# Another order of the instructions in layer 1's merged stage, and the last pair chosen in two halves

## The chip, the core and the metric

The kernel runs on one core of a Trainium2 chip. The metric is the device time of one execution in microseconds. The core has five engines that run their own instruction lists in order and meet only at semaphores: TensorE (PE in the rows, PEld for its weight loads), VectorE (DVE), ScalarE (ACT), GpSimd (POOL) and SyncE (SP). A semaphore wait stops everything queued behind it on its engine.

## The reference, cut to what matters

The program is two transformer-like layers with adaptive layer norm on 2 x 2048 tokens of width 256. The change lies in the first half of layer 1, which computes, for each batch element:

```
h  = layernorm(x) * (1 + ca) + sa
xn = h / (rms(h) + 1e-8)
u, v = silu(xn @ u_w.T + u_b), silu(xn @ v_w.T + v_b)
y  = toeplitz_mix(v)               # mixes over the batch axis of size 2
x  = x + ga * ((u * y) @ o_w.T + o_b + h)
g  = layernorm(x) * (1 + cb) + sb
xn = g * rsqrt(mean(g*g) + eps) * ln_w
logits = xn @ Wg + bg              # 8 experts
the two largest logits of a token choose its experts; softmax of the two weighs them
```

The mixing runs over an axis of size 2 here, so each row of y is a sum of both batch elements' v with three numbers per channel. The experts' own products belong to the next stage. This stage ends by putting each token's row into two slots of x_slots, sorted by expert, and by zeros behind each expert's last row.

## The kernel before, in words

`layer1` is one stage of eight, all others unchanged. Its 4096 rows are cut into 8 blocks of 512 tokens (4 tiles of 128), and a pass `c` (0 to 3, `CPS` = 4, `LAST` = 3) handles a pair of blocks, one of each batch element: j = 2c and 2c + 1. Passes are software-pipelined by hand: during pass c each engine also does work for the pair before (`older`, normalising the new x, routing) and for the pair behind (`newer`, preparing xn). Each engine's list is written out in its own block, and this written order is what the change edits.

In pass c TensorE does sixteen `up` (q = 0 to 15; p_uv, two matmuls of 128x512 each; the first eight make v, the others u), then `down(c, 0)` and `down(c, 1)` (d_po, 16 matmuls of 128x256). Between them stand `turn(2, j)` (transposes of xn_all into l_pt for the logits), `scores(j)` (logits), `turn(1, j)` (transposes of l_xn for the next pass) and `ranks` (counts of chosen experts). l_pt is one buffer, so each `turn` waits for ScalarE's `copy` of the one before. `down(c, 1)` uses the same PSUM tile as `down(c, 0)` and waits until VectorE has added that into l_h (`taken`, L1653).

ScalarE does the sixteen `gate` (silu of p_uv into v_sb or u_sb, L1429), with `square_h`, `square_n` (sums of squares), `scale_h`, `scale_n` and `copy` between them. VectorE does `center_h` and `center_n` (the layer norms), `mean_square_h`, `mean_square_n`, `invert`, `weigh` (times ln_w), `blend` (builds y_sb of v_sb, L1629 and L1634), `open_gate` (times u, L1646), `take_logits`, `choose`, `place` (slots), `residual` and `spread` (the new x and its statistics). GpSimd takes the roots (`deviation`, `inverse_root`, `root_mean_square`), adds a bias to h (`bias_rows`, L1318) and scatters rows to x_slots by indirect DMA (L1333), 16 per pair. SyncE loads weights at the start and, when `tails` is known (L1786), writes ten pieces of zeros (L1304).

The waits that matter below: `blend(c)` needs gates 0 to 7; `down(c, n)` needs `open_gate(c, n)`; `ranks` needs `choose`; `place` needs `ranks`; `scores` of the last pair need `weigh`, `turn` and `copy`; `tails` needs the ranks' total. After the last pass the last pair is normalised, scored, ranked and scattered with nothing beside it.

## Time and profile before

| | us |
|---|---|
| median of 3 runs | 2784.06 (2782.41 to 2786.93) |
| profiled execution | 2783.49 |
| its span | 2781.7 |
| the four passes of the stage (1605 to 1877) | 272.1 |
| from there to the next stage's first load (1948.5) | 71.4 |

Over the whole span TensorE is busy 82%, VectorE 61%, ScalarE 46% and GpSimd 27%, but these are averages over eight stages. The changed stage runs from about 1583 us to 1948 us of the span. The rows below are from its timeline, one engine at a time, and from its windows. A row of the timeline is: start in us, length in us, engine, line, operation, what is written and what is read, shapes and count, and in brackets how long the engine had stood idle before it and who released it.

### The profile page before, as it was taken

How to read it: one execution, taken by the hardware profiler on the slowest of the kernel's cores; microseconds unless marked ns; L12 is line 12 of the kernel's file. 1: busy time of each engine (PE TensorE's matmuls, PEld its weight loads, DVE VectorE, ACT ScalarE, POOL GpSimd, SP SyncE). 2: the span in 40 equal slices, each digit the busy share in tenths (PEclk: the TensorE clock that was granted, in tenths of full speed). 3: DMA queues.
4: the chain of work that ended last, by engine and by line, in shares of the span. 5: the costliest groups of instructions: out<-in, count | busy, mean ns of one | idle time of the engine just before them, and what ended most of it. 6: DMA issues, size and time to landing. Idle time of an engine off the chain costs nothing. (4 is left out here: it accounts for less than half of the span.)

```text
span 2781.7 us, 39688 instructions
## 1 busy us (share of the span) xinstructions
PE 2294.4 (82%) x13478; PEld 1450.0 (52%) x13478; DVE 1704.9 (61%) x2578; ACT 1276.2 (46%) x2419; POOL 750.3 (27%) x600
## 2 busy tenths in 40 slices
PE   3982899999999999997699677782799999999940
PEld 1771333333333333333577544452688888888840
DVE  4777867777666767752688757664355554545544
ACT  1330365666656676674233233321455555555520
POOL 2456001011010100000455411434233332323346
PEclk8995799999999999999899888895899999999975
DMA  4348906062442600001100100002443443443324
GB/s 157 119 145 130 254 6 144 5 142 29 118 50 98 115 2 2 2 2 43 53 0 0 29 0 1 31 31 98 169 171 122 146 150 124 136 160 120 128 63 130
DMA packets 139297, 238.37 MB, mean 86 GB/s; under 512 B 14960, under 2 KB 101744, under 8 KB 137712
## 3 DMA queue, kind: packets, MB, share of 16 engines
q1 hardware_dynamic: 113680, 147.43, 16.5%
q0 software_dynamic: 25440, 88.62, 13.6%
q8 instruction: 106, 1.74, 0.3%
q14 instruction: 71, 0.58, 0.1%
HBM read 150.94 MB, written 85.07 MB: 85 GB/s over the span
## 5 line engine op out<-in xcount | busy, mean ns | idle before, releaser
L819 DVE TENSOR_REDUCE tile_max<-p_m 128x2 f32<-128x1024 f32 (+3 forms) x640 | 650.2, 1060 | 258.8 <-PE p_m L654 164.3
L783 ACT ACTIVATE probs<-p_s 128x512 f32<-128x512 f32 (+3 forms) x1280 | 612.0, 529 | 357.3 <-PE p_s L667 202.0
L1959 PE MATMUL p_up<-f_xT,f_w 128*128 128x512 f32 (+1 forms) x2304 | 469.1, 352 | 8.9 <-POOL f_w L2089 8.9
L667 PE MATMUL p_s<-qa,ka 99*128 99x512 bf16 (+3 forms) x1280 | 387.0, 362 | 30.3 <-DMA qa<-max_scr 10.9
L654 PE MATMUL p_m<-ka,qa 96*128 96x512 bf16 (+3 forms) x1280 | 344.9, 369 | 74.8 <-DVE tile_max L819 39.3
L1959 PEld LDWEIGHTS p_up<-f_xT,f_w 128*128 128x128 f32 x2304 | 372.4, 189 | 62.4 <-issue 9.3
L2089 POOL TENSOR_TENSOR f_w<-f_raw,f_w 128x1024 fp32r<-128x1024 f32 x96 | 230.9, 2411 | 499.6 <-ACT f_w L2011 499.6
L682 PE MATMUL p_o<-probs,va 128*32 128x512 f32 (+3 forms) x2560 | 308.8, 552 | 4.3 <-issue 3.7
L667 PEld LDWEIGHTS p_s<-qa,ka 99*128 99x128 bf16 x1280 | 112.4, 98 | 371.6 <-ACT probs L783 297.9
L1974 PE MATMUL p_y<-f_w,f_hidden 128*128 128x256 f32 x1872 | 261.6, 286 | 22.8 <-DVE f_y L2065 11.4
L1974 PEld LDWEIGHTS p_y<-f_w,f_hidden 128*128 128x128 f32 x1872 | 240.9, 188 | 45.1 <-issue 23.2
L2053 DVE SCALAR_TENSOR_TENSOR f_gate<-p_up,f_b,f_gate 128x512 f32<-128x512 f32 (+1 forms) x192 | 124.5, 648 | 220.1 <-ACT f_gate L2024 219.9
L654 PEld LDWEIGHTS p_m<-ka,qa 96*128 96x128 bf16 x1280 | 121.1, 101 | 214.2 <-DVE tile_max L819 87.5
L2057 DVE TENSOR_TENSOR f_hidden<-f_gate,f_hidden 128x512 fp32r<-128x512 f32 (+1 forms) x192 | 137.9, 718 | 118.7 <-ACT f_hidden L2029 118.7
L2024 ACT ACTIVATE f_gate<-p_up,f_b 128x512 f32<-128x512 f32 (+1 forms) x192 | 116.2, 605 | 184.4 <-PE p_up L1959 168.7
L1088 PE MATMUL p_e<-w_expert,c_hT 128*128 128x512 f32 x768 | 195.3, 404 | 0.0
L595 POOL DMA_DIRECT2D qa<-qk_scr x42 | 21.4, 510 | 610.3 <-PE p_o L682 594.8
L2029 ACT ACTIVATE f_hidden<-f_gate 128x512 fp32r<-128x512 f32 (+1 forms) x192 | 106.0, 552 | 152.4 <-DVE f_gate L2053 149.6
L1088 PEld LDWEIGHTS p_e<-w_expert,c_hT 128*128 128x128 f32 x768 | 140.8, 190 | 29.6
L2011 ACT ACTIVATE f_w<-f_raw 128x1024 fp32r<-128x1024 f32 x144 | 150.4, 1045 | 6.1 <-DMA f_raw<-in_W1b 4.2
L258 POOL TENSOR_TENSOR rstd<-ve,neghalf 128x32 f32<-128x32 f32 x2 | 10.9, 5463 | 408.0 <-DVE ve L241 408.0
L1497 PE MATMUL p_uv<-l_xnT,w_uv 128*128 128x512 f32 x256 | 114.9, 607 | 0.0
(241 smaller groups left out, 2803.5 us busy)
## 6 DMA issues: line engine op xcount, KB each, us to landing
y_slots<-zeros POOLq DMA_DIRECT2D x73, 512.0 KB, 31.4
f_raw<-in_W1a SPq DMA_DIRECT2D x24, 1024.0 KB, 6.5
f_raw<-in_W1b SPq DMA_DIRECT2D x24, 1024.0 KB, 8.7
f_raw<-in_W SPq DMA_DIRECT2D x24, 1024.0 KB, 11.1
qk_scr<-parts SPq DMA_DIRECT2D x48, 256.0 KB, 2.3
qa<-qk_scr POOLq DMA_DIRECT2D x42, 256.0 KB, 15.6
ka<-qk_scr POOLq DMA_DIRECT2D x42, 256.0 KB, 18.2
v_scr<-va SPq DMA_DIRECT2D x32, 256.0 KB, 3.0
```

Of the source, the lines that this page charges most:

```text
L654: last = nc.tensor.matmul(p_m[:, u % 2, hh, 0:width], qa[0:QROWS, buf, hd, q0:q0 + P], ka[0:QROWS, buf, hd, bank * CH:bank * CH + width], ...
L667: last = nc.tensor.matmul(p_s[:, h % 2, lo:CH], ka[0:QROWS + SPLIT, buf, h, j * P:(j + 1) * P], qa[0:QROWS + SPLIT, buf, h, c * CH + lo:(c ...
L682: last = nc.tensor.matmul(p_o[VW * h:VW * (h + 1), lo:CH], va[:, buf, j, VW * h:VW * (h + 1)], probs[:, n % 2, h, lo:CH], start=j == 0, st ...
L783: nc.scalar.activation(probs[:, n % 2, h, lo:CH], p_s[:, h % 2, lo:CH], ACT.Exp, scale=DH ** -0.5).then_inc(probs_ready, 1)
L819: nc.vector.tensor_reduce(out=tile_max[:, 2 * hp:2 * hp + 2, i, bank], in_=p_m[:, u % 2, :, 0:width], op=ALU.max, axis=AX.X).then_inc(max_ ...
L1088: last = nc.tensor.matmul(out, hT[:, par, hp, kt, :], weights(wp, kt), start=(kt, wp, hp) == (0, HI, HI), stop=(kt, wp, hp) == (KT - 1, LO ...
L1959: last = nc.tensor.matmul(p_up[:, f % 2, ab, 0:size], w1[:, wh, ab * KT + kt, f * P:(f + 1) * P], xT[:, t % 2, xh, kt, 0:size], start=(kt, ...
L1974: last = nc.tensor.matmul(p_y[:, u, :], hidden[:, f % 2, hh, u * P:(u + 1) * P], w2[:, wh, f, :], start=(f, wh, hh) == (0, HI, HI) and u % ...
L2011: nc.scalar.activation(piece_part(q, HI), piece_raw(q, par), ACT.Copy).then_inc(w_high, 1)
L2053: nc.vector.scalar_tensor_tensor(out=gate[:, f % 2, 0:size], in0=p_up[:, f % 2, 1, 0:size], scalar=b1[:, t % 2, FB + f:FB + f + 1], in1=ga ...
L2057: nc.vector.tensor_tensor(hidden[:, f % 2, LO, 0:size], gate[:, f % 2, 0:size], hidden[:, f % 2, HI, 0:size], ALU.subtract).then_inc(hidde ...
L2089: nc.gpsimd.tensor_tensor(piece_part(q, LO), piece_raw(q, t % 2), piece_part(q, HI), ALU.subtract).then_inc(w1_ready, 1)
```

## The change

No arithmetic changes. In the passes:

- VectorE: `center_n(2c)` moves from the start of the following pass to the end of pass c, between the two residuals; `blend(c)` moves ahead of `mean_square_h(newer + 1)`, `invert` and `weigh(older + 1)`; `residual(c, 0)` and its `spread` move ahead of `place(c - 1)`; `take_logits` moves behind both `open_gate`.
- TensorE: `turn(2, older)` moves from q = 12 to q = 9 and its `scores` from the end of the `up` to q = 12; the odd block's turn and scores come behind all `up`; `turn(1, newer)` comes ahead of `down(c, 0)`, and `turn(1, newer + 1)` behind `ranks`.
- ScalarE: squares, scalings and copies stand behind other gates (see the diff).
- GpSimd: roots ahead of scatters; `deviation(2c)` at the end of pass c.

After the last pass the last pair is chosen in two groups, one per block: `choose`, `ranks` and `place` run for 4 tiles each (`groups` 3 and 4) in place of once for 8. The odd block's logits go to a part of p_uv, since l_small is written by the first group's ranks meanwhile.

```
--- before.py
+++ after.py
+        p_l_last = p_uv[:, 0, 0:TPC * E1].rearrange("p (u e) -> p u e", u=TPC)
...
+        groups = [(c, 0, B) for c in range(LAST)] + [(LAST, 0, 1), (LAST, 1, B)]
+        G = len(groups)
...
+        def p_logits(j):
+
+            return p_l_last if j == 2 * LAST + 1 else p_l[:, j % 2, :, :]
...
-                def scatter(c, lo, hi):
+                def scatter(g, lo, hi):
+                    c, n0, n1 = groups[g]
+                    size = (n1 - n0) * TPC
                     for s in range(lo, hi):
-                        q, n, u = s // PAIR, s % PAIR // TPC, s % TPC
+                        q, n, u = s // size, n0 + s % size // TPC, s % TPC
                         t = (n * CPS + c) * TPC + u
-                        pool.wait_ge(slots_ready, 2 * c + q + 1)
+                        pool.wait_ge(slots_ready, 2 * g + q + 1)
...
-                    older, newer = c - 1, c + 1
+                    older, newer = 2 * (c - 1), 2 * (c + 1)
                     if older >= 0:
-                        deviation(2 * older)
-                        deviation(2 * older + 1)
+                        deviation(older + 1)
+                        inverse_root(older)
                         if older:
-                            scatter(older - 1, 0, 3)
-                        inverse_root(2 * older)
-                        if older:
-                            scatter(older - 1, 3, 5)
-                        inverse_root(2 * older + 1)
-                        if older:
-                            scatter(older - 1, 5, 7)
-                    if newer < CPS:
-                        root_mean_square(2 * newer)
-                        if older > 0:
-                            scatter(older - 1, 7, 9)
-                        root_mean_square(2 * newer + 1)
+                            scatter(c - 2, 0, 8)
+                        inverse_root(older + 1)
+                    if newer < 2 * CPS:
+                        root_mean_square(newer)
                     if older > 0:
-                        scatter(older - 1, 9 if newer < CPS else 7, 2 * PAIR)
-                    if newer < CPS:
-                        bias_rows(2 * newer)
-                        bias_rows(2 * newer + 1)
-                deviation(2 * LAST)
+                        scatter(c - 2, 8, 12)
+                    if newer < 2 * CPS:
+                        root_mean_square(newer + 1)
+                    if older > 0:
+                        scatter(c - 2, 12, 2 * PAIR)
+                    if newer < 2 * CPS:
+                        bias_rows(newer)
+                        bias_rows(newer + 1)
+                    deviation(2 * c)
                 deviation(2 * LAST + 1)
-                scatter(LAST - 1, 0, 4)
                 inverse_root(2 * LAST)
+                scatter(LAST - 1, 0, 6)
                 inverse_root(2 * LAST + 1)
-                scatter(LAST - 1, 4, 2 * PAIR)
-                scatter(LAST, 0, 2 * PAIR)
+                scatter(LAST - 1, 6, 2 * PAIR)
+                scatter(LAST, 0, PAIR)
+                scatter(LAST + 1, 0, PAIR)
...
-                            if q == 5:
+                            if q == 2:
                                 square_n(older)
-                            if q == 7:
+                            if q == 6:
+                                scale_n(older)
+                            if q == 9:
+                                copy(2, older)
+                            if q == 11:
                                 square_n(older + 1)
-                            if q == 9:
-                                scale_n(older)
-                            if q == 11:
+                            if q == 14:
                                 scale_n(older + 1)
-                            if q == 12:
-                                copy(2, older)
-                            if q == 14:
-                                copy(2, older + 1)
                         if newer < 2 * CPS:
-                            if q == 10:
+                            if q == 8:
                                 square_h(newer)
                             if q == 13:
                                 square_h(newer + 1)
                     if newer < 2 * CPS:
                         scale_h(newer)
+                    if older >= 0:
+                        copy(2, older + 1)
+                    if newer < 2 * CPS:
                         scale_h(newer + 1)
                         copy(1, newer)
                         copy(1, newer + 1)
-                for j in (2 * LAST, 2 * LAST + 1):
-                    square_n(j)
-                for j in (2 * LAST, 2 * LAST + 1):
-                    scale_n(j)
-                for j in (2 * LAST, 2 * LAST + 1):
-                    copy(2, j)
+                square_n(2 * LAST)
+                scale_n(2 * LAST)
+                square_n(2 * LAST + 1)
+                copy(2, 2 * LAST)
+                scale_n(2 * LAST + 1)
+                copy(2, 2 * LAST + 1)
...
-                    if j >= B:
+                    if j == 2 * LAST + 1:
+                        pe.wait_ge(uv_ready, NB * CPS)
+                    elif j >= B:
                         pe.wait_ge(ranked, j // B)
                     for u in range(TPC):
                         for kt in range(KT):
-                            last = nc.tensor.matmul(p_l[:, j % 2, u, :], zT[:, j % 2, kt, u * P:(u + 1) * P],
+                            last = nc.tensor.matmul(p_logits(j)[:, u, :], zT[:, j % 2, kt, u * P:(u + 1) * P],
...
                     for q in range(NB):
                         up(c, q)
                         if older >= 0:
+                            if q == 9:
+                                turn(2, older)
                             if q == 12:
-                                turn(2, older)
-                            if q == 14:
-                                turn(2, older + 1)
+                                scores(older)
                     if older >= 0:
-                        scores(older)
+                        turn(2, older + 1)
                         scores(older + 1)
-                    down(c, 0)
                     if newer < 2 * CPS:
                         turn(1, newer)
-                        turn(1, newer + 1)
+                    down(c, 0)
                     if older >= 0:
                         ranks(c - 1)
+                    if newer < 2 * CPS:
+                        turn(1, newer + 1)
                     down(c, 1)
                 turn(2, 2 * LAST)
                 scores(2 * LAST)
                 turn(2, 2 * LAST + 1)
                 scores(2 * LAST + 1)
                 ranks(LAST)
-                pe.wait_ge(ranked, CPS)
-                nc.tensor.matmul(p_total, ones[:, :], cum[:, CPS % 2, :], start=True, stop=True).then_inc(total_ready, 1)
+                ranks(LAST + 1)
+                pe.wait_ge(ranked, G)
+                nc.tensor.matmul(p_total, ones[:, :], cum[:, G % 2, :], start=True, stop=True).then_inc(total_ready, 1)
 
...
+                def choose(g):
+
+                    c, n0, n1 = groups[g]
+                    size, lo, hi = (n1 - n0) * TPC, n0 * TPC, n1 * TPC
+                    if g == 0:
...
+                def place(g):
+                    c, n0, n1 = groups[g]
+                    size = (n1 - n0) * TPC
+                    dve.wait_ge(counted, g + 1)
...
                 for c in range(CPS):
                     older, newer = 2 * (c - 1), 2 * (c + 1)
                     if older >= 0:
-                        center_n(older)
-                        center_n(older + 1)
+                        mean_square_n(older)
                     if newer < 2 * CPS:
                         center_h(newer)
                     if older >= 0:
-                        mean_square_n(older)
+                        weigh(older)
+                        center_n(older + 1)
                     if newer < 2 * CPS:
                         center_h(newer + 1)
                     if older >= 0:
                         mean_square_n(older + 1)
                     if newer < 2 * CPS:
                         mean_square_h(newer)
-                    if older >= 0:
-                        weigh(older)
+                    blend(c)
                     if newer < 2 * CPS:
                         mean_square_h(newer + 1)
                         invert(newer)
                     if older >= 0:
                         weigh(older + 1)
+                    open_gate(c, 0)
                     if newer < 2 * CPS:
                         invert(newer + 1)
-                    blend(c)
+                    open_gate(c, 1)
                     if older >= 0:
                         take_logits(older)
-                    open_gate(c, 0)
-                    if older >= 0:
                         take_logits(older + 1)
-                    open_gate(c, 1)
-                    if older >= 0:
                         choose(c - 1)
-                        place(c - 1)
                     residual(c, 0)
                     spread(2 * c)
+                    if older >= 0:
+                        place(c - 1)
+                    center_n(2 * c)
                     residual(c, 1)
                     spread(2 * c + 1)
-                center_n(2 * LAST)
+                mean_square_n(2 * LAST)
                 center_n(2 * LAST + 1)
-                mean_square_n(2 * LAST)
+                weigh(2 * LAST)
                 mean_square_n(2 * LAST + 1)
-                weigh(2 * LAST)
+                take_logits(2 * LAST)
+                choose(LAST)
                 weigh(2 * LAST + 1)
-                take_logits(2 * LAST)
+                place(LAST)
                 take_logits(2 * LAST + 1)
-                choose(LAST)
-                place(LAST)
-
+                choose(LAST + 1)
+                place(LAST + 1)
```

TensorE in the second pass (c = 1), before: from the `up` (p_uv, two matmuls each) to the turns for the next pass. l_pt with xn_all is `turn(2, ...)`, l_pt with l_xn is `turn(1, ...)`, l_small with l_wl is `scores`, d_po is `down`.

```order
L1497 MATMUL p_uv<-l_xnT,w_uv 128x512 x26
L1487 MATMUL l_pt<-ident,xn_all 128x128 x8
L1497 MATMUL p_uv<-l_xnT,w_uv 128x512 x4
L1487 MATMUL l_pt<-ident,xn_all 128x128 x8
L1497 MATMUL p_uv<-l_xnT,w_uv 128x512 x2
L1520 MATMUL l_small<-l_wl,l_zT 128x8 x16
L1508 MATMUL d_po<-w_o,y_sb 128x256 x16
L1487 MATMUL l_pt<-ident,l_xn 128x128 x16
```

The same place now:

```order
L1505 MATMUL p_uv<-l_xnT,w_uv 128x512 x20
L1495 MATMUL l_pt<-ident,xn_all 128x128 x8
L1505 MATMUL p_uv<-l_xnT,w_uv 128x512 x6
L1530 MATMUL l_small<-l_wl,l_zT 128x8 x8
L1505 MATMUL p_uv<-l_xnT,w_uv 128x512 x6
L1495 MATMUL l_pt<-ident,xn_all 128x128 x8
L1530 MATMUL l_small<-l_wl,l_zT 128x8 x8
L1495 MATMUL l_pt<-ident,l_xn 128x128 x8
L1516 MATMUL d_po<-w_o,y_sb 128x256 x16
```

The first turn is three `up` earlier with its scores three `up` behind it, the second turn and its scores stand behind all `up`, and only one of the turns for the next pass is left ahead of the first `down` (the other is behind the ranks).

VectorE in the second pass, before: l_ms is `mean_square`, xn_all `weigh`, y_sb with v_sb `blend`, y_sb with u_sb `open_gate`, l_logits `take_logits`.

```order
L1603 TENSOR_SCALAR l_ms<-l_ss 128x4
L1577 TENSOR_SCALAR l_rms<-l_rms 128x4
L1613 RECIPROCAL l_inv<-l_rms 128x4
L1620 TENSOR_TENSOR xn_all<-xn_all,l_ln 128x1024
L1577 TENSOR_SCALAR l_rms<-l_rms 128x4
L1613 RECIPROCAL l_inv<-l_rms 128x4
L1629 TENSOR_SCALAR y_sb<-v_sb,toep 128x512 x8
L1634 SCALAR_TENSOR_TENSOR y_sb<-v_sb,toep,y_sb 128x512 x8
L1678 TENSOR_TENSOR l_logits<-l_small,l_bl 128x32
L1646 TENSOR_TENSOR y_sb<-y_sb,u_sb 128x2048
L1678 TENSOR_TENSOR l_logits<-l_small,l_bl 128x32
L1646 TENSOR_TENSOR y_sb<-y_sb,u_sb 128x2048
```

The same place now:

```order
L1617 TENSOR_SCALAR l_ms<-l_ss 128x4
L1643 TENSOR_SCALAR y_sb<-v_sb,toep 128x512 x8
L1648 SCALAR_TENSOR_TENSOR y_sb<-v_sb,toep,y_sb 128x512 x8
L1617 TENSOR_SCALAR l_ms<-l_ss 128x4
L1591 TENSOR_SCALAR l_rms<-l_rms 128x4
L1627 RECIPROCAL l_inv<-l_rms 128x4
L1634 TENSOR_TENSOR xn_all<-xn_all,l_ln 128x1024
L1660 TENSOR_TENSOR y_sb<-y_sb,u_sb 128x2048
L1591 TENSOR_SCALAR l_rms<-l_rms 128x4
L1627 RECIPROCAL l_inv<-l_rms 128x4
L1660 TENSOR_TENSOR y_sb<-y_sb,u_sb 128x2048
```

`blend` moved ahead of the second mean square, `invert` and `weigh`, and the logits behind the second `open_gate`.

TensorE behind the last `down`, before (turns, scores, ranks of eight tiles):

```order
L1508 MATMUL d_po<-w_o,y_sb 128x256 x16
L1487 MATMUL l_pt<-ident,xn_all 128x128 x8
L1520 MATMUL l_small<-l_wl,l_zT 128x8 x8
L1487 MATMUL l_pt<-ident,xn_all 128x128 x8
L1520 MATMUL l_small<-l_wl,l_zT 128x8 x8
L1531 MATMUL l_small<-r_chosen,r_later 128x64
L1533 MATMUL l_small<-r_chosen,r_ones 128x56
```

And now:

```order
L1516 MATMUL d_po<-w_o,y_sb 128x256 x16
L1495 MATMUL l_pt<-ident,xn_all 128x128 x8
L1530 MATMUL l_small<-l_wl,l_zT 128x8 x8
L1495 MATMUL l_pt<-ident,xn_all 128x128 x8
L1530 MATMUL p_uv<-l_wl,l_zT 128x8 x8
L1543 MATMUL l_small<-r_chosen,r_later 128x32
L1545 MATMUL l_small<-r_chosen,r_ones 128x24
L1545 MATMUL l_small<-r_chosen,r_ones 128x16
L1545 MATMUL l_small<-r_chosen,r_ones 128x8
L1547 MATMUL l_small<-r_cum,r_ones 128x32
L1543 MATMUL l_small<-r_chosen,r_later 128x32
```

The ranks are cut in two groups of four tiles, and the second scores go to p_uv.

## Rows read from the trace of the kernel before

**Rows 1.** Windows by pass: us, busy of PE, PEld, DVE, ACT, POOL; clock, DMA, GB/s.

```profile
1605.00:1670.60 65.60, 48.58 (x148) 29.02 (x147) 30.30 (x46) 21.38 (x44) 8.13 (x6) 0.84 0.00 0
1670.60:1743.50 72.90, 55.23 (x212) 36.03 (x211) 51.82 (x103) 27.16 (x68) 12.71 (x8) 0.88 0.00 1
1743.50:1818.40 74.90, 56.81 (x211) 36.39 (x211) 52.53 (x103) 27.27 (x68) 30.28 (x24) 0.86 0.08 29
1818.40:1877.10 58.70, 52.67 (x195) 34.04 (x193) 40.05 (x86) 18.85 (x42) 23.38 (x20) 0.91 0.11 37
1877.10:1948.50 71.40, 15.62 (x68) 14.45 (x68) 34.14 (x107) 10.16 (x28) 34.68 (x35) 0.53 0.27 96
```

**Rows 2.** Timeline of TensorE, first pass.

```profile
1605.23 29.37 PE L1497 MATMUL p_uv<-l_xnT,w_uv 128*128 128x512 f32 x64
1650.41 10.17 PE L1508 MATMUL d_po<-w_o,y_sb 128*128 128x256 f32 x32 [15.82 <-DVE y_sb L1646]
...
1663.56 7.07 PE L1508 MATMUL d_po<-w_o,y_sb 128*128 128x256 f32 x32
```

**Rows 3.** Timelines of ScalarE, VectorE and GpSimd, first pass.

```profile
1622.62 0.69 ACT L1429 ACTIVATE u_sb<-p_uv,b_uv 128x512 f32<-128x512 f32 x1 [1.03 <-PE p_uv L1497]
...
1626.05 0.69 ACT L1429 ACTIVATE u_sb<-p_uv,b_uv 128x512 f32<-128x512 f32 x1 [1.03 <-PE p_uv L1497]
...
1628.23 0.67 ACT L1429 ACTIVATE u_sb<-p_uv,b_uv 128x512 f32<-128x512 f32 x1
...
1635.22 3.29 ACT L1392 ACTIVATE l_xn<-l_h,l_inv 128x256 f32<-128x256 f32 x8
...
1633.51 0.17 DVE L1603 TENSOR_SCALAR l_ms<-l_ss 128x4 f32<-128x4 f32 x1 [4.98 <-ACT l_squares L1384]
...
1635.10 7.40 DVE L1629 TENSOR_SCALAR y_sb<-v_sb,toep 128x512 f32<-128x512 f32 x8
...
1636.99 4.83 POOL L1318 TENSOR_TENSOR l_h<-l_h,l_ob 128x1024 f32<-128x1024 f32 x2 [2.23 <-ACT l_xn L1392]
```

**Rows 4.** Timeline of TensorE, second and third pass.

```profile
1704.31 3.73 PE L1520 MATMUL l_small<-l_wl,l_zT 128*128 128x8 f32 x32
1717.14 9.24 PE L1508 MATMUL d_po<-w_o,y_sb 128*128 128x256 f32 x32 [9.11 <-DVE y_sb L1646]
1726.22 1.04 PE L1487 MATMUL l_pt<-ident,l_xn 128*128 128x128 f32 x8
...
1734.66 8.83 PE L1508 MATMUL d_po<-w_o,y_sb 128*128 128x256 f32 x32 [3.17 <-DVE l_h L1653]
1743.33 22.48 PE L1497 MATMUL p_uv<-l_xnT,w_uv 128*128 128x512 f32 x52
...
1768.80 5.29 PE L1497 MATMUL p_uv<-l_xnT,w_uv 128*128 128x512 f32 x8
```

**Rows 5.** Timeline of VectorE, second and third pass.

```profile
1717.11 2.28 DVE L1646 TENSOR_TENSOR y_sb<-y_sb,u_sb 128x2048 f32<-128x2048 f32 x1
...
1731.59 0.22 DVE L1710 TENSOR_TENSOR r_run<-l_small,r_table 128x64 f32<-128x64 f32 x1 [8.74 <-PE l_small L1535]
...
1776.25 3.29 DVE L1629 TENSOR_SCALAR y_sb<-v_sb,toep 128x512 f32<-128x512 f32 x8
1779.57 5.40 DVE L1634 SCALAR_TENSOR_TENSOR y_sb<-v_sb,toep,y_sb 128x512 f32<-128x512 f32 x8
```

**Rows 6.** Timelines of TensorE, VectorE, GpSimd and SyncE after the last pass.

```profile
1895.68 1.97 PE L1487 MATMUL l_pt<-ident,xn_all 128*128 128x128 f32 x8 [18.62 <-DVE xn_all L1620]
...
1912.79 3.10 PE L1533 MATMUL l_small<-r_chosen,r_ones 128*128 128x56 f32 x14
...
1919.38 0.17 DVE L1786 CAST tails<-r_tail_f 128x8 int32<-128x8 f32 x1
...
1936.95 0.96 POOL L1333 DMA_INDIRECT x_slots<-xn_all,slots  x1 [0.30 <-issue]
...
1920.66 16.11 SPq L1304 DMA_DIRECT2D x_slots<-u_sb  x10
```

77 lines of the change are left out of this document (37 added, 40 removed).

## Prediction, made before the changed kernel ran

> **What bounds the kernel now.** I read the windows first, cut where TensorE ends the second output product of a pass. The four passes over the chunk pairs last 65.6, 72.9, 74.9 and 58.7 us, and 71.4 us follow until the next stage's first load [rows 1]. No engine fills a pass: in the second TensorE is busy 55.2 us of 72.9, VectorE 51.8, ScalarE 27.2. So a pass is a chain through engines that wait for each other, and the order of instructions sets its length.
>
> TensorE's timeline shows where it stands still. In the first pass it waits 15.82 us for y_sb before `down` [rows 2]; in the second 9.11 us at the same place, and then 3.17 us before the second `down`, for l_h of VectorE [rows 4]. The third pass repeats both, the fourth the second one and a shorter first.
>
> VectorE's timeline says why y_sb is late. Its input v_sb is complete after the eighth `gate`, but `blend`, which builds y_sb, stands behind `mean_square_h` of the next pair's second half, whose squares ScalarE does only after gate 13. VectorE waits 4.98 us there in the first pass [rows 3] and longer in the next two. The 3.17 us are order too: `place(c-1)` waits 8.74 us for TensorE's ranks [rows 5], and `residual(c, 0)`, whose add frees p_o for the second `down`, stands behind it.
>
> After the last pass the first weighed rows reach TensorE 18.62 us after its last `down`. Then turn, scores, ranks and place run one after the other at half clock; `tails` is written at 1919.5, SyncE's ten zero writes go out from 1920.7 to 1936.8, and GpSimd's last scatter ends at 1937.9 [rows 6]. The next load follows at 1948.5: 71.4 us after the passes.
>
> **The change part by part.** The sum goes against the profiled execution: 2783.49 us (span 2781.7), close to the median of 2784.06. Between engines I count 0.2 us from TensorE's end to a reader and 0.05 elsewhere, as the starts in the rows stand to each other.
>
> Durations. One `up` is 22.48 / 13 = 1.72 us, a `turn` 1.0 at full clock and 1.97 at half, a `down` 7.0, two `scores` 3.73, so one 1.85 [rows 2, 4, 6]. Fourteen rank instructions took 3.10 at half clock, so all eighteen 4.0, and 2.05 at full [rows 6]. `gate` and four squares take ScalarE from 1626.05 to 1628.23, 2.2 us, of which the squares are 1.6; eight scalings take 3.29 [rows 3]; a copy is 1.0. `blend` is 3.29 + 5.40 = 8.7, `open_gate` 2.3, an add or product of half its width 1.2 [rows 5].
> Nothing is added in the passes but order. The last pair's `choose` and `place` run twice at half width, 24 more VectorE instructions in all, and its ranks are 2 x 5 matmuls in place of 9.
>
> First pass. Squares move to gates 8 and 13, and `blend` now waits for the first only. Gate 8 starts at 1622.62, so the squares end at 1624.8, `blend` at 1633.6, and the first `open_gate`, with 0.5 us of small work ahead of it, at 1636.4. TensorE is through its `up` at 1605.23 + 29.37 = 1634.6; `turn(1, 2)` needs xn, which is scaled from 1635.2 on, so it ends at 1637.9. `down` ends at 1644.9: the wait of 15.82 is gone. `residual`'s add ends at 1646.3, `turn(1, 3)` beside it, the second `down` at 1653.3. Before it was 1663.56 + 7.07 = 1670.6: 17.3 us less.
>
> Second and third pass, from T, the end of the `down` before. ScalarE's squares for `mean_square_n(older + 1)` follow gate 11: twelve `up` (20.6), a `turn` (1.0), 0.2 and 2.2 give T + 24.0. VectorE is there at T + 23.3: rest of `residual` and `spread` to T + 8, `center_h` 3.8, a wait for the scaling behind gate 6 until T + 14.4, `weigh` 1.2, `center_n` and `center_h` 3.8 each less small overlaps. Then `blend` 8.7, 0.6 of small work, `weigh(older + 1)` 1.2: T + 34.6. TensorE has done sixteen `up`, a turn and one `scores` at T + 30.3, so a new wait of 4.3 us stands here. The turn behind it I take at half clock, 1.9: T + 36.5. Copy 1.2, `scores` 1.95, `turn(1, newer)` 1.0: T + 40.6. `down` 7.0, ranks 2.05, turn 0.9, `down` 7.0: T + 57.5. `open_gate(c, 0)`, from T + 34.6, hides behind copy and scores; `residual`'s add hides behind ranks and turn, so the 3.17 are gone. Gain: 72.9 - 57.5 = 15.4 and 74.9 - 57.5 = 17.4.
>
> Fourth pass, without a newer pair: `weigh(5)` at T + 34.0, turn 35.9, copy and scores 39.1, `down` 46.1, ranks 48.1, `down` 55.1, against 58.7: 3.6.
> Sum of the passes: 17.3 + 15.4 + 17.4 + 3.6 = 53.7 us.
>
> What follows the passes loses. From D, the end of the last `down`: VectorE now has `place` and `center_n(6)` between the residuals, so `spread(7)` ends at D + 8.8, about 3 later than before. `center_n(7)` to 13.8, `weigh(6)` 15.0, turn 17.0, copy 18.1, `scores` at half clock 3.6, 21.7; the half-width `choose` to 25.1 and only behind it `weigh(7)` 26.3, turn 28.2, copy 29.4, scores 33.0, ranks of the first half (5/9 of 4.0) 35.4, its `place` and the second `choose` 39.9, ranks 42.4, `place`, a memset and tails 45.4. Before it was 1919.5 - 1877.1 = 42.4. So tails come 3.0 us later after D. SyncE then needs 1.1 us to its first write and 16.1 to its last [rows 6], D + 62.6. GpSimd's last scatter ends at D + 57.4: eight from D + 36.9 and eight behind them, 1.27 us each. Before, the two were level. So the early half of the scatters is worth nothing, because SyncE's writes decide.
>
> GpSimd's `bias_rows` holds VectorE up: beside its 4.83 us the first part of `blend` took 7.40 in place of 3.29, 4.1 more [rows 3, 5]. It moves from `blend` to `open_gate` and `choose`; at 4.1 us the `choose` ends at T + 47.3, just ahead of ranks at T + 47.6, so it is covered to 0.3 us. If it cost twice that, each of passes two and three would lose about 4.
> The Trainium skill (SBUF — State Buffer, "SBUF: two separate sides") calls this an exclusive lock, held for the whole instruction and only against some VectorE operations. By that rule the small operations of `choose` could escape it and nothing would be lost; the trace shows no `choose` beside `bias_rows`.
>
> Clock. The wait of 3.17 us before `down` goes with 8.83 us for it in place of 7.07, and one near 2 us goes with two `up` of 5.29 in place of 3.4 to 3.6 [rows 2, 4]: about 1.7 us each. I have half clock on one turn only. Bounds: nothing more, or 1.7 us in each of passes two to four, 5.1. I take the middle, 2.5, since waits near 2 us did both.
>
> Total: -53.7 + 3.0 + 2.5 = -48.2, and 2783.5 - 48.2 = 2735 us.
>
> **Rivals.** (A) VectorE becomes the bound and part of the waits returns. For: it is busy 51.8 us per pass, and with the gaps between its instructions my pass of 57.5 leaves it some 3 us. Another 4 us in each of three passes give 12 back: 2747. Against: where it waits now it has nothing else to do, and that work is only moved.
> (B) Better: TensorE stays at full clock behind the 4.3 us, and after the passes too. There two turns, two scores and the ranks take half, 7 us less, the turns of the passes 2, and no allowance, 2.5: 2724. Against: the stretch after the passes had 0.53 granted [rows 1].
> (C) Slower: the clock falls at the new wait of each pass and stays low to the end of the pass. Behind it lie 0.95 + 1.85 + 0.95 + 7 + 2.05 + 0.95 + 7 = 20.8 us at full clock, of which the sum has the turn at half already: 19.8 more in three passes, 59.4, less the 2.5 of allowance: 2792. It decides once the low level lasts some 16 us in a pass. Against: after 9.11 us of waiting `down` took 9.24, 2.2 more, and the turn behind it 1.04, full clock [rows 4].
> The Trainium skill (TensorE: Matmul & The Clock Gate, "What's actually happening") says that the throttled state is the default and activity releases it; by that rule the new waits make (C) possible and the work behind them ends it, as the rows say.
> (D) The change does not do what it says: ScalarE's `copy(2, older)` now stands behind gate 9 and holds the later gates if `weigh(older)` is late, until the passes are as long as before: 2784. Against: `weigh(older)` is there at T + 15.6 and the turn is due at T + 17.2, a margin of 1.6 us; it would have to be late by some 16.
>
> **Numbers.** Forecast, with its own range 2727 to 2743: 0.65. (A), up to 2757: 0.20. (B), below 2727: 0.09. (C) 0.04, (D) 0.02. The range that leaves out no more than two in ten is 2726 to 2751. A difference of 0.2%, 5.6 us, is what a measurement of this kernel can tell. From the same cases: faster 0.94, within it 0.02, slower 0.04.
>
> **What would show it.** Right: no wait near 16 us in the first pass, whose second `down` ends near 1653; passes two and three of 57 to 58 us with one wait of about 4 us, before `turn(2, older + 1)`; no wait for l_h before a second `down`; tails about 45 us after the last `down`; SyncE's writes end after the scatters. Wrong: gates that lag so that `up` waits; a wait for y_sb before `down` above 2 us; a granted clock below 0.85 in the passes; tails later than D + 48.

## The result, and the profile after

The changed kernel takes 2738.5 us (2734.6 to 2740.6, four runs) against 2784.5 us (2782.4 to 2786.9, four runs) of the kernel before: a ratio of 0.983, 95% interval 0.982 to 0.985, or 46 us less. The forecast was 2735 us, with a range of 2726 to 2751. Below, "stage" is the time from the first turn of layer 1's merged stage to the next stage's first load, and D is again the end of the last `down`.

The windows of the kernel after, by pass, cut at the same places as [rows 1] (columns: stretch, length, busy time and count of TensorE, its weight loads, VectorE, ScalarE, GpSimd, then granted clock, DMA share, GB/s):

```profile
1600.90:1649.10 48.20, 45.29 (x147) 26.84 (x146) 27.14 (x50) 21.27 (x44) 9.72 (x6) 0.97 0.00 1
1649.10:1709.00 59.90, 54.74 (x212) 36.80 (x211) 51.88 (x105) 27.27 (x68) 13.26 (x8) 0.91 0.00 1
1709.00:1769.50 60.50, 55.13 (x211) 36.90 (x211) 52.46 (x104) 27.27 (x68) 29.82 (x24) 0.92 0.10 35
1769.50:1828.70 59.20, 54.44 (x194) 35.55 (x192) 38.67 (x85) 18.96 (x42) 26.27 (x20) 0.88 0.11 36
1828.70:1898.60 69.90, 16.24 (x71) 14.95 (x70) 35.74 (x125) 10.39 (x28) 35.59 (x35) 0.53 0.28 98
```

The first three passes are 17.4, 13.0 and 14.4 us shorter, and the fourth, for which 3.6 us less had been forecast, is 0.5 longer; what follows them is 1.5 shorter. In the second and third pass VectorE does the same 52 us of work in 60 us instead of 73 to 75, which is where the time came from: idle between instructions, not work. From first turn to load the stage lost 45.8 us (348.2 to 302.4), which is the difference of the medians. The two profiled executions differ by 48.9 us; the other 3 are in stages that the change doesn't touch (the stage begins 4.1 us earlier in the one after, and what follows it is 0.9 longer).

TensorE's timeline in the first, second and fourth pass of the kernel after, which answers to [rows 2, 4]:

```profile
1632.56 1.09 PE L1495 MATMUL l_pt<-ident,l_xn 128*128 128x128 f32 x8 [2.37 <-ACT l_xn L1399]
1633.49 7.07 PE L1516 MATMUL d_po<-w_o,y_sb 128*128 128x256 f32 x32
...
1673.85 5.40 PE L1505 MATMUL p_uv<-l_xnT,w_uv 128*128 128x512 f32 x12
1683.30 1.97 PE L1495 MATMUL l_pt<-ident,xn_all 128*128 128x128 f32 x8 [4.05 <-DVE xn_all L1634]
1686.38 3.58 PE L1530 MATMUL l_small<-l_wl,l_zT 128*128 128x8 f32 x16 [1.11 <-ACT l_zT L1427]
1689.81 1.95 PE L1495 MATMUL l_pt<-ident,l_xn 128*128 128x128 f32 x8
1691.55 7.69 PE L1516 MATMUL d_po<-w_o,y_sb 128*128 128x256 f32 x32
...
1701.91 7.07 PE L1516 MATMUL d_po<-w_o,y_sb 128*128 128x256 f32 x32
...
1803.23 1.97 PE L1495 MATMUL l_pt<-ident,xn_all 128*128 128x128 f32 x8 [3.65 <-DVE xn_all L1634]
1806.31 3.58 PE L1530 MATMUL l_small<-l_wl,l_zT 128*128 128x8 f32 x16 [1.11 <-ACT l_zT L1427]
1809.74 10.08 PE L1516 MATMUL d_po<-w_o,y_sb 128*128 128x256 f32 x32
```

The waits of 15.82 and 9.11 us for y_sb and of 3.17 us for l_h are gone. One wait of about 4 us has come, before the older pair's second turn (4.05, 4.26 and 3.65 us in passes two to four). Read the lengths behind it: the turn takes 1.97 us and not 1.04 (1.42 in the third pass), the scores 3.58 and not 1.85, the next turn 1.95, and the first `down` 7.69, 8.64 and 10.08 us against 7.07 for the second. TensorE runs at its lower clock level there, 1.2 GHz, and comes back to 2.4 within the `down`: in the second pass the granted clock is 0.91 in the four microseconds before the turn, 0.50 from the turn to the start of the `down`, 0.84 in the first half of the `down` and 1.00 in the second.

VectorE's timeline after has no wait of `place` for the ranks any more (8.74 us in [rows 5]); `place` starts in a row of small instructions behind `spread`. GpSimd's `bias_rows` shows in two places (VectorE and GpSimd, second pass):

```profile
1683.16 2.28 DVE L1660 TENSOR_TENSOR y_sb<-y_sb,u_sb 128x2048 f32<-128x2048 f32 x1
1683.95 3.69 POOL L1326 TENSOR_TENSOR l_h<-l_h,l_ob 128x1024 f32<-128x1024 f32 x1 [1.01 <-ACT l_xn L1399]
1685.36 2.31 DVE L1591 TENSOR_SCALAR l_rms<-l_rms 128x4 f32<-128x4 f32 x1
...
1689.70 2.58 POOL L1326 TENSOR_TENSOR l_h<-l_h,l_ob 128x1024 f32<-128x1024 f32 x1 [2.06 <-ACT l_xn L1399]
1689.99 0.29 DVE L1692 TENSOR_TENSOR l_logits<-l_small,l_bl 128x32 f32<-128x32 f32 x2
1690.38 0.22 DVE L1705 TENSOR_REDUCE r_best<-l_logits 128x8 f32<-128x64 f32 x1
1690.64 1.73 DVE L1587 TENSOR_TENSOR r_same<-l_logits,r_best 128x64 f32<-128x64 f32 x1
```

A 128x4 instruction that takes 0.16 us elsewhere took 2.31, and one of 128x64 took 1.73 instead of 0.22 (4.82 in the third pass); each ends with GpSimd's addition.

The ending of the kernel after (TensorE, GpSimd and SyncE), which answers to [rows 6]:

```profile
1843.67 1.97 PE L1495 MATMUL l_pt<-ident,xn_all 128*128 128x128 f32 x8 [14.94 <-DVE xn_all L1634]
...
1868.40 0.64 PE L1543 MATMUL l_small<-r_chosen,r_later 128*128 128x32 f32 x2 [4.50 <-DVE r_chosen L1715]
...
1884.12 0.96 POOL L1343 DMA_INDIRECT x_slots<-xn_all,slots  x1 [0.30 <-issue]
...
1875.07 17.54 SPq L1312 DMA_DIRECT2D x_slots<-u_sb  x10
...
1898.61 0.40 SPq L1917 DMA_DIRECT2D f_x<-x_slots  x1
```

SyncE's first write comes at D + 46.3 (D + 43.6 before), the last scatter ends at D + 56.3 (60.9 before), SyncE's last issue at D + 63.9 (59.7 before), and the load comes at D + 69.9 (71.5 before).

### The profile page after: what moved, and what is told of

Read it like the earlier page. It is cut to its first block and busy times, and to the rows that moved or that the text cites. A ratio compares the mean times of both kernels' runs of the same rounds, so it can differ in the third digit from the quotient of the medians.

```text
span 2732.7 us, 39713 instructions
## 1 busy us (share of the span) xinstructions
PE 2290.5 (84%) x13480; PEld 1450.9 (53%) x13480; DVE 1702.5 (62%) x2599; ACT 1276.7 (47%) x2419; POOL 756.8 (28%) x600
## 5 line engine op out<-in xcount | busy, mean ns | idle before, releaser
L654 PE MATMUL p_m<-ka,qa 96*128 96x512 bf16 (+3 forms) x1280 | 344.5, 369 | 73.2 <-DVE tile_max L819 39.5
L476 PE MATMUL p_qk<-hT,wqkv 128*128 128x512 f32 x384 | 99.0, 417 | 18.4 <-DVE rot L390 16.0
```

Source lines behind the costliest of these rows:

```text
L654: last = nc.tensor.matmul(p_m[:, u % 2, hh, 0:width], qa[0:QROWS, buf, hd, q0:q0 + P], ka[0:QROWS, buf, hd, bank * CH:bank * CH + width], ...
```

## The experiments

Theory after the result: the mechanism is the forecast's; the clock's fall behind the new wait was undersized; and in the ending of the kernel before it was GpSimd's last scatters, not SyncE's zeros, that held the load back. The rivals: VectorE's holds beside `bias_rows` (rival A of the prediction) are what stands in the passes; the clock's fall has nothing to do with the new wait; SyncE decides the ending in both kernels.

**e1_first_pass**: the kernel before, with only the first pass's `blend` and squares moved.

```
-                            if q == 10:
+                            if q == (10 if c else 8):
                                 square_h(newer)
...
+                    if c == 0:
+                        blend(c)
                     ... (as before)
+                    if c:
                         blend(c)
```

> The kernel before with two edits, both for pass 0 alone: square_h(newer) behind gate 8 in place of 10, and blend(0) ahead of mean_square_h(newer + 1). Theory (order on VectorE made the 15.8 us wait): pass 0 takes 48.2 us as in the changed kernel in place of 65.6, all later passes as before, so -17.4 us, ratio 0.9938. Rival (the gain needs the other moves too, since turn(1, 2) and turn(1, 3) still stand between the two products): pass 0 ends about 2 us later than that, -15 us. Rival (VectorE gives it back in pass 1): under -8 us.

Measured: 2767.3 us, ratio 0.994 (0.992 to 0.996), 17 us less. The first pass goes from 70.3 to 55.0 us (counted from the first turn), the other three stay within 0.4 us. So 15.3 of the 17.4 us come from these two edits alone, as the first rival had it. The other 2.1 come only with the rest of the change, in which a turn stands ahead of the first `down`: here TensorE waits 2.95 us for y_sb and that `down` takes 8.86 us, while in the kernel after it waits 2.37 us, turns, and needs 7.07. The ending is 1.7 us longer than before (see e4_ending_order), so the stage is 14.1 us shorter in the trace; the medians' 16.8 is not exact enough to choose between the expectations, the trace is.

**e2_residual_first**: the kernel before, with `residual(c, 0)` and `spread(2c)` ahead of `place(c - 1)` alone.

```
-                        place(c - 1)
                     residual(c, 0)
                     spread(2 * c)
+                    if older >= 0:
+                        place(c - 1)
```

> The kernel before with one edit: residual(c, 0) and its spread ahead of place(c - 1) on VectorE. Theory (the wait of 3.2 us before the second product costs its own length and, by the half clock behind it, another 1.7): three passes lose 4.9 us each, -15 us, ratio 0.9947, and the second product takes 7.07 in place of 8.8. Rival (the clock falls anyhow, since the product follows 9 us of waiting): 3.2 each, -9.6 us. Rival (place comes later and the next pass waits for it): no change.

Measured: 2766.2 us, ratio 0.993 (0.991 to 0.995), 18 us less, from two lines. The last three passes are 5.1, 10.2 and 4.5 us shorter. TensorE in its second pass:

```profile
1720.25 9.21 PE L1508 MATMUL d_po<-w_o,y_sb 128*128 128x256 f32 x32 [9.05 <-DVE y_sb L1646]
...
1734.39 7.13 PE L1508 MATMUL d_po<-w_o,y_sb 128*128 128x256 f32 x32
...
1785.06 9.23 PE L1508 MATMUL d_po<-w_o,y_sb 128*128 128x256 f32 x32 [6.05 <-DVE y_sb L1646]
```

The 3.17 us before the second `down` are gone and with them its half clock (8.83 to 7.13): that is the 5.1. In the next pass VectorE comes earlier too, and the wait for y_sb shrinks to 6.05 us. In the kernel before the same row is:

```profile
1792.02 9.35 PE L1508 MATMUL d_po<-w_o,y_sb 128*128 128x256 f32 x32 [9.70 <-DVE y_sb L1646]
```

Two `up` of that pass take 3.60 us and not 5.29 as well, which completes the 10.2. A stall on VectorE that looks local (8.74 us in `place`) was paid twice.

e2 leaves 7.9 and 4.3 us of the second and third pass to the rest of the change; no run moves `blend` alone there, so that part is read from the waits that are gone. In the fourth pass the rest of the change costs: e2 takes 54.1 us and the kernel after 59.3. In e2 TensorE waits 2.56 us before the first `down`, in the kernel after 3.65 us before the turn, with half clock behind it.

**e3_filled_wait**: the kernel after, with four matmuls of 128x512 that nobody reads ahead of the turn that waits.

```
+                        pe.wait_ge(copied, turn_no[2, older + 1])
+                        for _ in range(4):
+                            nc.tensor.matmul(p_t[:, 0, :], w[:, 0, 0:P], xnT[:, c % 2, 0, 0, :], start=True, stop=True)
                         turn(2, older + 1)
```

> The changed kernel with four matmuls of 128x512 (two passes each, 3.4 us at full clock) ahead of turn(2, older + 1) in passes 1 to 3; their result is overwritten unread. They fill most of the new wait of 3.7 to 4.3 us. Theory (the passes are longer than forecast because TensorE runs at half clock behind this wait): turn, scores and turn run at full clock, passes take 56.6, 56.6 and 54.1 in place of 59.9, 60.5 and 59.2, in all -12 us against the changed kernel. Rival (the clock falls for another reason, or falls again at the 1.1 us wait for the copy): -0 to -3 us. Rival (the added matmuls themselves delay the turn): up to +3 us.

Measured: 2735.8 us (2.7 less than after, within the spread); in the trace the stage is 296.3 us against 302.4, half of the 12 us expected. The passes are 53.0, 59.2, 58.4 and 55.6 us. TensorE in its second pass:

```profile
1685.31 3.60 PE L1565 MATMUL l_pt<-l_xnT,w_uv 128*128 128x512 f32 x8
1689.52 1.09 PE L1495 MATMUL l_pt<-ident,xn_all 128*128 128x128 f32 x8 [0.62 <-DVE xn_all L1637]
1691.73 3.09 PE L1530 MATMUL l_small<-l_wl,l_zT 128*128 128x8 f32 x16 [1.12 <-ACT l_zT L1427]
1694.67 1.95 PE L1495 MATMUL l_pt<-ident,l_xn 128*128 128x128 f32 x8
1696.41 8.41 PE L1516 MATMUL d_po<-w_o,y_sb 128*128 128x256 f32 x32
```

With the wait down from 4.05 to 0.62 us the turn is at full clock, but the fall still comes, one product later. The long wait is a part of the cause, not all of it.

**e8_two_fills**: six such matmuls in that place and ten of 128x64 between the turn and its scores.

```
+                        for _ in range(6):
+                            nc.tensor.matmul(p_t[:, 0, :], w[:, 0, 0:P], xnT[:, c % 2, 0, 0, :], start=True, stop=True)
                         turn(2, older + 1)
+                        if c > 1:
+                            pe.wait_ge(ranked, c - 1)
+                        for _ in range(10):
+                            nc.tensor.matmul(p_rank[:, 0:2 * TPC, :].rearrange("p a e -> p (a e)"), w[:, 0, 0:P],
+                                             xnT[:, c % 2, 0, 0, 0:2 * TPC * E1], start=True, stop=True)
                         scores(older + 1)
```

> The kernel after with idle TensorE filled in two places of passes 2 to 4: six matmuls of 128x512 whose result nobody reads before the turn of the older pair's second block, and ten of 128x64 between that turn and its scores (where 1.1 us of waiting for the copy stood). With four fillers in the first place alone the stage took 296.3 us against 302.4 and the granted clock still fell behind the remaining waits of 0.6 to 1.5 and 1.1 us. Theory (what the forecast missed is the half clock behind the wait): scores, turn and first down product now run at the full clock throughout (1.85, 1.04, 7.07 us instead of 1.95 to 3.09, 1.85 to 1.95, 8.0 to 8.8), -3.4, -1.9 and about -2 us, stage 289 to 291. Rival (the clock's fall doesn't hang on these waits, the load before them sets it): the down products stay at 8 us and more and the stage stays at 296, or gets longer by the fillers that reach past the wait (0.3 us each pass).

Measured: 2733.1 us (2728.2 to 2744.1, which settles nothing); the stage 299.4 us, 3 longer than with four fillers. TensorE in its second pass, with no wait left in it:

```profile
1677.67 5.31 PE L1565 MATMUL l_pt<-l_xnT,w_uv 128*128 128x512 f32 x12
1682.82 1.04 PE L1495 MATMUL l_pt<-ident,xn_all 128*128 128x128 f32 x8
1683.70 2.34 PE L1570 MATMUL l_small<-l_xnT,w_uv 128*128 128x64 f32 x20
1685.88 2.28 PE L1530 MATMUL l_small<-l_wl,l_zT 128*128 128x8 f32 x16
1688.01 1.95 PE L1495 MATMUL l_pt<-ident,l_xn 128*128 128x128 f32 x8
1689.75 9.21 PE L1516 MATMUL d_po<-w_o,y_sb 128*128 128x256 f32 x32
```

The rival expected this. TensorE works without a break, and the clock falls in the scores all the same: the work before it was a turn, ten products of 64 columns and the scores, all of them short products. In the third pass it falls one product later (scores 1.90, turn 1.92, `down` 7.94 us), and in the fourth, where no newer pair's turn follows, the `down` takes 7.15. The same turn and scores in the middle of the `up` products (1.04 and 1.85 us, in every pass) never show a fall. So the run of short work between the last `up` and the first `down` can lower the clock by itself, and the 4 us wait in front of it makes the fall come sooner. The expectation had the six reach 0.3 us past the wait. At 0.9 us each (5.31 for six, 3.60 for four) they outlasted it by about 1 us, and the ten by another: the passes' gain went there.

**e7_bias_8_columns**: the kernel after, with `bias_rows` on 8 of 256 columns. It leaves out most of the addition of the output bias.

```
-                    rows = h[:, j // B % 2, j % B, :, :]
+                    rows = h[:, j // B % 2, j % B, :, 0:8]
```

> The kernel after with GpSimd's bias addition cut from 256 columns to 8 in each row (it leaves out most of the addition of the output bias in this stage). It tells whether VectorE's share of memory ports with GpSimd costs anything on the path: two small instructions of VectorE were held 2.31 and 1.73 us beside that addition, and the blend's two additions took 3.25 and 5.39 us in the first pass. My account: these lie beside TensorE's up products and the stage keeps its 302.4 us within 1. Rival (VectorE is what the centring waits for, so its holds are in the 3.7 to 4.3 us wait before the turn): the holds of about 2 to 3 us go from that wait in passes 2 to 4, the half clock behind it gets shorter too, and the stage is 6 to 12 us shorter.

Measured: 2740.5 us (2736.6 to 2741.5), stage 302.6 us against 302.4. VectorE and TensorE in its second pass:

```profile
1689.53 1.97 PE L1495 MATMUL l_pt<-ident,xn_all 128*128 128x128 f32 x8 [4.06 <-DVE xn_all L1634]
...
1691.60 0.22 DVE L1591 TENSOR_SCALAR l_rms<-l_rms 128x4 f32<-128x4 f32 x1
```

The hold of 2.31 us is gone (0.22) and the wait before the turn is what it was (4.05, now 4.06). Rival A's price for it is zero in this order: VectorE's holds lie where nobody waits for it. In e9 and e10 below they don't.

The runs of unchanged passes also show how exact the clock's price is. The kernel after and e7 take 60.5 and 59.3 us in the third and fourth pass; e4_ending_order and e5_no_halves, whose passes are the same, take 61.1 and 56.9. In the fourth pass the wait is 3.65 us in all of them, but in e4 and e5 the turn behind it is still at full clock (1.09) and the first `down` takes 8.60 and 8.54 us, not 10.08.

**e6_halves_only**: the kernel before, with the last pair chosen in two halves.

> The kernel before with the after-kernel's ending alone (the last pair chosen in two halves, its scatters in two groups); the passes stay at about 70.3, 72.9, 75.0 and 58.6 us. Tails about D+47, SyncE's zeros from about D+47 to D+64.5, GpSimd's last scatter ends about D+57. By the later-of-two-ends theory (GpSimd + 10.6, SyncE + 6.0) the load comes at D+70.5, against 71.5 before: -1 us, no difference that this can measure. By my prediction (SyncE's start alone decides, +3.0): load D+74.5 and 3 us slower (2787).

Its edit is the part of the change behind the last pass (`groups`, `p_l_last`, the order of `weigh`, `take_logits`, `choose`, `place` there, and ScalarE's and GpSimd's order there). Measured: 2785.6 us, ratio 1.0005 (0.9989 to 1.0021): nothing. SyncE's first write at D + 48.4, its last issue at D + 66.0, the last scatter's end at D + 58.5, the load at D + 72.0 (71.5 before), where the prediction's account had 74.5.

**e5_no_halves**: the kernel after, with the last pair chosen once.

```
-        groups = [(c, 0, B) for c in range(LAST)] + [(LAST, 0, 1), (LAST, 1, B)]
+        groups = [(c, 0, B) for c in range(CPS)]
```

> The kernel after with its last pair chosen and ranked once, as before; the passes are untouched and keep about 52.9, 59.9, 60.5 and 59.3 us. D is the end of the last down product. The ranks come one choose and one rank later than the half ones but nothing is split: the tails are ready about D+40, SyncE's ten writes of zeros begin about D+41 (D+46.3 in the kernel after) and end D+58; GpSimd's last sixteen scatters start together and end about D+58.2 (D+56.3 in the kernel after). Theory now: the next stage's load waits for the later of two ends, GpSimd's last issue + 10.6 us and SyncE's last issue + 6.0 us, as in the five profiles read so far; then the load comes at D+68.8, against 69.9 in the kernel after, and the time is about 1 us shorter (2737.5). Rival, the one of my prediction: SyncE's zeros decide and the early half of the scatters is worth nothing; then the load comes at D+64 to 65 and the time is about 5 us shorter (2733).

Measured: 2738.8 us (2737.8 to 2739.5), the kernel after's own time. SyncE and GpSimd in its ending (D is 1831.6):

```profile
1873.68 19.01 SPq L1311 DMA_DIRECT2D x_slots<-u_sb  x10
1901.90 0.41 SPq L1910 DMA_DIRECT2D f_x<-x_slots  x1
...
1889.96 0.96 POOL L1342 DMA_INDIRECT x_slots<-xn_all,slots  x1 [0.30 <-issue]
```

SyncE starts 4.2 us earlier after D than in the kernel after and is through 2.8 earlier (the ten writes took 19.0 us and not 17.5); the last scatter ends 3.0 later, and the load comes at D + 70.3, 0.4 later. If SyncE alone decided, the load would have come at D + 67.1, 6.0 behind its end (64 to 65 with the end that was expected). Together with the earlier runs:

| kernel | scatters end | SyncE ends | load | scatters + 10.6 | SyncE + 6.0 |
|---|---|---|---|---|---|
| before | D + 60.9 | 59.7 | 71.5 | **71.5** | 65.7 |
| after | 56.3 | 63.9 | 69.9 | 66.9 | **69.9** |
| e1_first_pass | 62.6 | 63.7 | 73.2 | **73.2** | 69.7 |
| e4_ending_order | 58.2 | 66.4 | 72.4 | 68.8 | **72.4** |
| e5_no_halves | 59.3 | 61.1 | 70.3 | **69.9** | 67.1 |
| e6_halves_only | 58.5 | 66.0 | 72.0 | 69.1 | **72.0** |

The two constants are read off the first two rows; the load of the four others lies within 0.4 us of the later of the two ends (so do those of e2, e3 and e7 to e10). It is not the transfers that take longer on GpSimd's side: in the kernel before the last packet of the scatters is through at 1939.3, 1.4 us behind the last issue, and the load comes 9.2 us after that; in the kernel after SyncE's last packet is through at 1894.7 and the load comes 3.9 us after. What GpSimd still does in those 9.2 us before the next stage can begin, no view shows; that it is GpSimd's side is inferred from the four kernels in which that end is the later one (before, e1, e2, e5).

**e4_ending_order**: the kernel after, with `weigh(7)` ahead of `place`, ScalarE's copy behind its scaling, and four more of the pair before's scatters moved behind GpSimd's second root.

```
-                scatter(LAST - 1, 0, 6)
+                scatter(LAST - 1, 0, 2)
...
-                scatter(LAST - 1, 6, 2 * PAIR)
+                scatter(LAST - 1, 2, 2 * PAIR)
...
+                weigh(2 * LAST + 1)
                 take_logits(2 * LAST)
                 choose(LAST)
-                weigh(2 * LAST + 1)
                 place(LAST)
```

> The changed kernel with another ending: inverse_root(7) behind two scatters in place of six, scale_n(7) ahead of copy(2, 6), weigh(7) ahead of the first choose. Theory (in the ending the second half waits for weigh(7), which stands behind six scatters and a choose): tails come 42.1 us after the last product in place of 45.2, the next stage's load 66.7 in place of 69.9, -3.2 us. Rival (GpSimd's scatters set the end, whatever tails do): the load moves with the last scatter only, -5 us if slots of the first half come 3 us earlier, else 0. Rival (scores(6) are delayed by copy behind scale_n and this cancels it): 0.

Measured: 2742.5 us, ratio 0.984 (0.980 to 0.989), the load at D + 72.4: a miss, the load comes 2.5 us later than in the kernel after instead of 3.2 earlier. TensorE, GpSimd and VectorE:

```profile
1866.03 0.61 PE L1547 MATMUL l_small<-r_cum,r_ones 128*128 128x32 f32 x2
...
1868.48 0.96 POOL L1343 DMA_INDIRECT x_slots<-xn_all,slots  x1 [0.30 <-issue]
1871.93 0.19 DVE L1726 TENSOR_TENSOR r_run<-l_small,r_table 128x32 f32<-128x32 f32 x1 [10.61 <-remote]
```

The ranks were there at 1866.6, and VectorE's `place` began 5.3 us later, without an instruction between, 2.5 us behind the last of the pair's scatters (1869.4). In the kernel after the same step began at once (0.04 us behind the ranks), its scatters being through 1.8 us before. e1_first_pass and e2_residual_first show a smaller delay of the kind, 1.8 us from the scores to `take_logits`, 1.2 us behind the last scatter of the string, and their load comes 1.7 us later after D than before; but in the kernel before VectorE took over at once beside the same string. What holds VectorE there is not settled; the profile names only "remote".

**e9_early_weigh** and **e10_early_choice**: the short run behind the wait can't be filled cheaply, so make the row earlier. ScalarE scales the older pair's second block one gate earlier and copies its turn before it scales h; VectorE weighs it inside `blend`; in e10 the choice also comes before the second `open_gate`.

```
-                            if q == 14:
+                            if q == 13:
                                 scale_n(older + 1)
...
-                            if q == 13:
+                            if q == 14:
                                 square_h(newer + 1)
...
+                            if c and (f, n) == (1, 0):
+                                weigh(2 * c - 1)
...
-                        weigh(older + 1)
...
+                    if older >= 0:
+                        copy(2, older + 1)
                     if newer < 2 * CPS:
                         scale_h(newer)
-                    if older >= 0:
-                        copy(2, older + 1)
```

and in e10 alone:

```
-                    open_gate(c, 1)
                         take_logits(older)
                         take_logits(older + 1)
                         choose(c - 1)
+                    open_gate(c, 1)
```

> The kernel after with the block that TensorE waits for made earlier instead of filled: in passes 2 to 4 ScalarE scales the older pair's second block one gate earlier and copies its turn before it scales h of the newer pair, and VectorE weighs it after three of the blend's eight additions instead of behind all of them. From after's second pass: the turn starts at about +0.6 us behind the up products instead of +4.05; scores, the newer turn and the first down product then wait for VectorE's gate multiplication (ready 1685.44 in the profile after, down began 1691.55), so the down can start 6 us earlier; the ranks behind it then wait 2 to 3 us for the choice, which VectorE ends at 1695.3 whatever TensorE does. Theory: -3.5 us in each of three passes, less up to 1 us each if the clock falls behind the new wait; stage 292 to 295 against 302.4, time 2728 to 2731. Rival (the wait for VectorE only moves on: it has the longest work of the pass and is what sets it): the stage keeps 300 to 302.

> The kernel of the run before it, and VectorE also makes the routing choice of the older pair before the second gate multiplication instead of behind it, so that the ranks find it ready (about 1690.8 against 1692.6, the down product's end). Theory: the ranks' wait of 2 to 3 us goes too, the second down follows 5.8 us earlier than in the kernel after, -5 to -6 us in each of three passes; stage 285 to 288, time 2720 to 2723. Rival: VectorE, busy 52.3 of a pass's 60 us, becomes the bound: passes no shorter than 54 to 56 us, waits for it stand before the downs, and the stage ends at 290 to 294, no better than the run before it by more than 2 us.

Measured: e9 2728.7 us (2724.5 to 2731.4), ratio 0.980 (0.979 to 0.982); stage 295.0 us. e10 2732.4 us (2727.1 to 2737.5), ratio 0.983 (0.981 to 0.984); stage 291.5 us. Their times don't rank the two. e9's lie below all of the kernel after's (2734.6 to 2740.6), though the two were measured at different times. e9 came out as its theory had it (292 to 295 and 2728 to 2731); e10 missed its theory (285 to 288) and lies in its rival's range (290 to 294). TensorE in e9's third pass:

```profile
1740.04 1.09 PE L1495 MATMUL l_pt<-ident,xn_all 128*128 128x128 f32 x8 [0.40 <-DVE xn_all L1634]
1742.25 1.95 PE L1530 MATMUL l_small<-l_wl,l_zT 128*128 128x8 f32 x16 [1.11 <-ACT l_zT L1427]
1745.46 1.97 PE L1495 MATMUL l_pt<-ident,l_xn 128*128 128x128 f32 x8 [1.26 <-ACT l_xn L1399]
1747.22 7.83 PE L1516 MATMUL d_po<-w_o,y_sb 128*128 128x256 f32 x32
1756.81 0.43 PE L1543 MATMUL l_small<-r_chosen,r_later 128*128 128x64 f32 x2 [1.76 <-DVE r_chosen L1717]
```

and the windows of e10's second and third pass:

```profile
1654.45:1710.45 56.00, 53.84 (x211) 35.71 (x211) 51.79 (x105) 27.12 (x68) 11.92 (x8) 0.94 0.00 1
1710.45:1766.80 56.35, 52.77 (x212) 34.67 (x211) 52.09 (x102) 27.12 (x68) 29.94 (x24) 0.97 0.11 38
```

The wait of 4 us is 0.40. In e9's third pass 1.76 us of it come back as a wait for the choice (2 to 3 us in each pass were expected; the second and fourth have none), and in e10 that wait is gone. VectorE and GpSimd in e9's third pass show where the 1.76 come from:

```profile
1751.16 5.34 DVE L1587 TENSOR_TENSOR r_onehot<-r_iota,r_first_at 128x64 f32<-128x64 f32 x1
1751.74 4.67 POOL L1326 TENSOR_TENSOR l_h<-l_h,l_ob 128x1024 f32<-128x1024 f32 x2
```

The comparison ends with `bias_rows`; at its usual 0.22 us the choice would have been ready about 3 us before the `down` ended (1755.05). In e10's third pass the second `open_gate` meets `bias_rows` and takes 7.46 us in place of 2.26, and the second `down` waits 0.80 us for l_h. So the holds that cost nothing in the kernel after reach the path once the order is better; no run takes `bias_rows` out of e9 or e10, so their whole price there isn't measured. e10's passes end at 56.0, 56.4 and 54.6 us. TensorE is busy over 93% of each, VectorE over 92% of the second and third (73% of the fourth), its holds counted in: there VectorE is near its bound, as rival A had it, and little is left in order alone. e9's first pass is 1.4 us longer than the kernel after's: the moved squares make the wait before the turn 2.89 us in place of 2.37, and the first `down` behind it takes 8.71 us and not 7.07.

## Why the prediction was right, and where it was not

- First pass: -17.3 forecast, -17.4 measured.
- `blend` and `residual` moved in passes two to four: mechanism right. The waits for y_sb and l_h are gone, each as named; e2 shows it alone for `residual`, the trace of the kernel after for `blend`. One wait stands in their place, where it was put and of its size (4.05, 4.26 and 3.65 us against 4.3).
- The clock behind it: the term that was mis-sized. The allowance was 2.5 us with 5.1 as the bound; passes two to four took 59.9, 60.5 and 59.3 us against bare sums of 57.5, 57.5 and 55.1, 9.6 us more. I had sized it by what one `down` lost behind a wait (1.7 us). But behind this wait came first a turn, scores and (in passes two and three) a turn, at the low level, scores at 3.58 us and not 1.85, before the `down` lost its 0.6 to 3.0 us. The fourth pass lost most, 4.2 us, more than the 3.6 that the sum had it gain. The bound should have been counted over all the short work up to the first long product. Even an exact size of the wait would not have given it: in e8 the clock also fell with no wait at all, and with the same passes e4 and e5 lost 7.9 and 7.8 us in place of 9.6.
- The Trainium skill (TensorE: Matmul & The Clock Gate, "What's actually happening") says that the low level is the default and that activity releases it. The trace of the kernel after agrees in that in each of passes two to four the fall ended within the first long `down`. e8 adds that short products without a break (turn 1.04, fillers 2.34 us) didn't hold the high level in its second pass.
- Ending: +3.0 us forecast, -1.6 measured. Tails were right (SyncE's first write +2.7). The step that failed is "the early half of the scatters is worth nothing, because SyncE's writes decide". In [rows 6] both engines end together, and I compared the ends of their issues. What is late in the kernel before is GpSimd's side, which lets the next stage begin 10.6 us behind its last issue against SyncE's 6.0. In the kernel after the scatters end 4.6 us earlier (3.0 of it by the halves, as e5 against it shows), SyncE takes over at +6.0, and the later tails cost nothing. Undone (e5) or alone (e6), the halves are worth nothing that can be measured.
- The two errors, +7.0 in the passes and -4.6 in the ending, nearly cancelled, and that is luck: the stage was forecast to lose 48.2 us and lost 45.8. The median is 3.5 us above the forecast for the same 2.4 and for the 1 us by which the median of the kernel before stands above the profiled time that the sum started from.
- Rival A (VectorE's bound, its holds): the holds have no price here (e7), and VectorE is near its bound only once the order is better than the one forecast (e9, e10). Rival C was right in its mechanism, half clock behind the new wait, but the fall ended within the first `down` and never reached 16 us of a pass. B and D didn't happen.

## What to carry to other kernels

When a reordering leaves one wait in place of several, price the clock over everything short that stands behind it until the next long product, not over the first instruction; and know that a run of short products alone can lower it (e8). Where two engines end a stage together, don't compare their last issues: here the next stage could begin 10.6 us behind GpSimd's last scatter and 6.0 behind SyncE's last write. Filling a wait with idle products gave half of what was hoped; moving up what it waits for gave 7 to 11 us of the stage. A hold that costs nothing in one order (e7) can stand on the path in the next (e9): look at it again after each reordering.
